# Grouping the 47th and 48th tile of nodes in a graph layer with eight experts

## What is computed

```python
hn = layernorm(x)
m = clifford_linear(hn[src] * r[edge_type]) * gate(r[edge_type]) * norm(deg_src[src], deg_dst[dst])
x = x + clifford_linear(hn + segment_sum(m, dst))
w = softmax(mean(layernorm(x)) @ Wr + br)        # the batch is one, so w is per node
y = sum over experts e of  w[e] * (relu(bn(relu(bn(layernorm(x) @ W1[e])) @ W2[e])) @ Wo[e] + bo[e])
x = x + y
```

## The kernel before

| pass | tiles | superblocks in it, at step |
|---|---|---|
| 22 | 2 | 182 to 185 at s0 to s3, 186 at s6, 187 at s9 |
| 23 | 2 | 188 at s1, 189 at s3, 190 at s6, 191 at s9 |
| 24 | 1 | 192 at s1, 193 at s3, 194 at s9 |
| 25 | 1 | 195 at s3 |
| 26 | 1 | none |

## Time and profile before

### The profile page before, as it was taken

One profiled execution on the slowest core, in us unless ns is written; L12 is line 12 of the kernel. 1 busy time (PEld: TensorE's weight loads), 2 busy tenths in 40 slices (PEclk: granted clock), 3 DMA queues, 4 the chain that ended last, 5 costly groups with the idle time before them and its releaser, 6 DMA issues.

```text
span 1869.9 us, 31246 instructions
## 1 busy us (share of the span) xinstructions
PE 1766.2 (94%) x10694; PEld 1602.7 (86%) x10694; DVE 1167.4 (62%) x2407; ACT 1310.4 (70%) x2960; POOL 1371.3 (73%) x1391
## 2 busy tenths in 40 slices
PE   5846889999999999999999999999999999999998
PEld 5835888888989989989989989998998998997888
DVE  8966566656656656656656666756665665665552
ACT  5546777768777767777768767777876776773455
POOL 5867777777777777777777777777777777777720
PEclk9977999999999999999999999999999999999999
DMA  8167344445444434434445435434444443433320
GB/s 252 52 248 229 101 135 133 109 127 136 114 117 133 127 104 131 130 105 132 126 108 135 127 107 132 129 104 129 134 115 117 133 126 105 135 109 106 105 45 6
DMA packets 93691, 231.21 MB, mean 124 GB/s; under 512 B 23338, under 2 KB 44838, under 8 KB 93595
## 3 DMA queue, kind: packets, MB, share of 16 engines
q0 software_dynamic: 60768, 168.61, 34.2%
q1 hardware_dynamic: 32012, 60.45, 10.5%
q10 hardware_dynamic: 815, 1.16, 0.2%
HBM read 216.69 MB, written 13.44 MB: 123 GB/s over the span
## 4 chain that ended last, share of the span: by engine, by line
POOL 57%; PE 19%; issue 18%; DVE 4%; DMA 2%; ACT 1%; DVEq 0%; POOLq 0%; SPq 0%
POOL H L458 36%; POOL R L458 21%; PE z L829 8%; PE y L853 4%; DVE H L1011 2%; PE pr L889 2%; PE y L740 2%; PE o L877 1%; DMA H<-h_table,src 1%; DMA h_table<-big 1%; ACT big L563 1%; PE y L805 0%; PE y L786 0%; DVE acc L1227 0%; DMA src<-in_src 0%
## 5 line engine op out<-in xcount | busy, mean ns | idle before, releaser
L458 POOL DMA_INDIRECT H<-h_table,src x784 | 817.5, 1043 | 248.3 <-issue 238.5
L458 POOL DMA_INDIRECT R<-r_table,typ x482 | 535.4, 1111 | 164.3 <-issue 163.7
L644 ACT ACTIVATE h<-z,bns 128x256 f32<-128x256 f32 (+1 forms) x864 | 418.5, 540 | 325.1 <-PE z L829 323.0
L1227 DVE SCALAR_TENSOR_TENSOR acc<-y,wg,acc 128x256 f32<-128x256 f32 x392 | 173.5, 480 | 476.3 <-PE y L853 475.1
L596 ACT ACTIVATE OH<-tb,iota_t 125x128 fp32r<-125x128 int32 x1208 | 383.7, 392 | 65.1 <-PE pr L889 49.9
L829 PE MATMUL z<-h,big 128*128 128x256 f32 (+1 forms) x1728 | 376.9, 362 | 3.2 <-ACT h L644 2.8
L829 PE MATMUL z<-hT,big 128*128 128x256 f32 (+1 forms) x1728 | 377.3, 362 | 0.7 <-ACT h L644 0.7
L853 PE MATMUL y<-big,h 128*128 128x256 f32 x1568 | 374.4, 380 | 1.7 <-DVE lg L1196 1.6
L889 PE MATMUL pr<-RH,OH 125*128 125x258 f32 x1208 | 334.8, 312 | 26.9 <-DVE H L1286 16.3
L829 PEld LDWEIGHTS z<-h,big 128*128 128x128 f32 x1728 | 306.7, 192 | 39.6 <-ACT h L644 4.4
L853 PEld LDWEIGHTS y<-big,h 128*128 128x128 f32 x1568 | 294.3, 191 | 38.8 <-issue 1.9
(11 more groups left out here) (166 smaller groups left out, 1511.9 us busy)
## 6 DMA issues: line engine op xcount, KB each, us to landing
tb<-in_typ_row SPq DMA_DIRECT2D x24, 728.0 KB
H<-h_table,src POOLq DMA_INDIRECT x784, 2.8
R<-r_table,typ POOLq DMA_INDIRECT x482, 2.8
h_table<-big SPq DMA_DIRECT2D x7, 910.0 KB, 8.6
big<-in_x SPq DMA_DIRECT2D x7, 896.0 KB, 10.9
big<-in_w SPq DMA_DIRECT2D x8, 768.0 KB, 4.8
acc<-in_x SPq DMA_DIRECT2D x22, 256.0 KB, 7.1
hxT<-in_xt SPq DMA_DIRECT2D x22, 256.0 KB
```

The source lines that it names most:

```text
L458: pool.indirect_dma_start(out=to[:, b * DX:(b + 1) * DX], out_offset=None, in_=tab, in_offset=bass.IndirectOffsetOnAxis(ap=ix[:, J * SB + ...
L644: last = s_.activation(o[:, m, 0:wide_], z_[:, m, 0:wide_], ACT.Relu, bias=bns[:, l, 1, c:c + 1], scale=bns[:, l, 0, c:c + 1])
L1227: last = v.scalar_tensor_tensor(out=acc[:, g % 3, t, :], in0=b[:, t * D:(t + 1) * D], scalar=wg[:, t, e_:e_ + 1], in1=acc[:, g % 3, t, :], ...
```

## The change

Two expressions in `sizes` change. The grouping condition `nt - t > 4` becomes `nt - t > 2`, so that tiles 46 and 47 are one group of two and only tile 48 is alone: 26 groups instead of 27. `WHOLE` becomes the end of the last group of two less one step of 8.

```diff
--- before.py
+++ after.py
@@ -32,7 +32,7 @@
     front = 2 if nt > 8 else 0
     groups, t = [], 0
     while t < nt:
-        w = 2 if t >= front and nt - t > 4 else 1
+        w = 2 if t >= front and nt - t > 2 else 1
         groups.append((t, w))
         t += w
 
@@ -56,7 +56,7 @@
         hi = max([t for t in range(nt) if edges(t, -1) < (2 * j + 2) * SE] + [lo])
         tiles.append((lo, hi))
     assert n < nt * P
-    whole = ends[twos[-1]] if twos else nsb
+    whole = max(ends[twos[-1]] - step, 0) if twos else nsb
     alike = [g for g in twos if g + 2 in twos and ends[g + 1] - ends[g] == step == ends[g + 2] - ends[g + 1]]
     loop = range(alike[0], alike[-1] + 1) if alike else range(0)
     loop = loop[:len(loop) // 2 * 2] if step % 4 == 0 else range(0)
```

## The result

The changed kernel takes **1900.77 us** (median of 4 runs, 1898.65 to 1906.57) against 1877.03 us (4 runs, 1874.71 to 1878.33): a ratio of 1.0137, 95% interval 1.0117 to 1.0157, so it is slower by 22 to 29 us. The prediction was 1904.4 us, with a range of 1897 to 1911.

What follows compares the result with a forecast made beforehand. POOL's gathers bound the tail: gate at 1794.0 + 28.3 + 46.7 + 27.8 = 1896.8 us against a span of 1869.9, +26.9; added to the median of 1877.46 this gave 1904.4 us, range 1897 to 1911.

Steps and rivals of the forecast that it cites:

- POOL is full with 73%: POOL's gathers cost 0.95 us plus an uncounted 0.30 us gap, so POOL at 73% busy practically never waits for buffers.
- The gate: Turned sums of group 24 in pass 23 wait for the gathers of superblock 195 and start at 1794.0 us.
- Rival B: POOL's slow gathers vanish where DVE is idle between landings, gate 7.0 us earlier: 1897.4 us; chance 0.12.
- the rule of shared interfaces: GpSimd and VectorE contend for SBUF; one more pair of two-input DVE operations among the gathers costs about 1 us: 1905.4 us.
- PE's idle time: In pass 23 PE waits five times for superblocks 190 to 193 and the turned sums: 29.6 us of new idle time.
- rival A: PE's clock stays at half (1.2 GHz) through the gated stretch and beyond: 1909.3 us; chance 0.16.
- Behind the gate: From the turned sums of group 24 to the next pass, now with one superblock: 28.3 us.
- the cold start: After the wait for the turned sums, 16 PE matmuls take 5.30 instead of 3.46 us, 1.84 us more.
- The pass of two and the last pass: The two-tile pass with one superblock takes 46.7 us; the last single pass and the store take 27.8 us.
- The saving of 5.0 us: Merging two one-tile passes into one of two tiles saves PE 5.0 us of its time, 53.3 less 48.3.
- Rival C: Gathers are hidden anyway and PE bounds, so only the saving of 5.0 us is left: 1872.5 us; chance 0.03.
- a slow stretch between the gates: PE's time between gates has 3 to 6 us of slack, so a stretch at slow clock there costs nothing.

Runs made afterwards that it cites:

- the kernel with the early demand alone: Kernel before, single tiles kept, but superblocks 192 and 193 demanded one group earlier, as in the changed kernel: ratio 1.0164, +30.7 us.
- the lean pair: Kernel before and changed kernel, each without the 40 relation gathers from superblock 186 on: ratios 0.9966 and 0.9959 to the kernel before.
- the run with the held product: Kernel before with DVE's product of superblock 187 and ACT's copy moved from s3 to s5 of pass 22: ratio 1.0000.

## Why the prediction was right

**The bound.** The step "POOL is full with 73%" carried everything, and the runs bear it out from both sides: 40 gathers fewer, -6.4 us; 3 more, +4.5 us (1.3 to 7.7).

**The gate.** Predicted 87.8 us behind the turned sums of group 23, measured 86.7. POOL's 64 gathers from the last one of superblock 187 to the last one of 195 took 1794.95 - 1709.56 = 85.4 us instead of 87.0:

```profile
1709.56 0.95 POOL L458 DMA_INDIRECT H<-h_table,src  x1 [0.30 <-issue]
...
1794.95 0.95 POOL L458 DMA_INDIRECT H<-h_table,src  x1 [0.30 <-issue]
```

The last landing took 4.10 us where the sum had 3.63, though the gather itself was not slow (0.95 us, where the sum had taken over 1.83): the 1.80 us from a gather's end to its landing, read from one gather, were 3.15 here. So the gate's 1.1 us are two errors of opposite sign, 1.6 us less for the gathers and 0.5 us more for the landing. Rival B (no slow gathers, 7.0 us earlier) is refuted as an extreme: 1.6 of the 7.0 us went. The 1 us that the rule of shared interfaces (the Trainium skill, GPSIMD Engine Reference, section 1, Specifications) would have added for one more product among the gathers did not appear; the total moved the other way.

**PE's idle time, a term off in kind.** Predicted: 29.6 us in five waits (11.2, 5.6, 3.2, 3.9, 5.7). Measured: 7.33, 3.49, 2.09, 3.46 and 3.28, 19.7 us, with the 1.59 before them 21.2 us. That is a third off, and by the prediction's own sign (an idle time far from 30 us) it counts against it. Of the 8.4 us missing, 1.1 are the earlier gate and the rest is slow work. The windows of PE busy, with granted clock in third place from the end:

```profile
1748.00:1803.00 55.00, 35.36 (x149) 29.57 (x148) 22.95 (x38) 14.10 (x23) 36.94 (x37) 0.84 0.40 99
1772.00:1787.00 15.00, 12.51 (x61) 10.37 (x59) 6.14 (x10) 4.03 (x7) 11.64 (x12) 1.00 0.40 110
1803.00:1830.00 27.00, 26.62 (x126) 23.09 (x125) 9.16 (x32) 11.42 (x21) 0.00 (x0) 0.94 0.00 1
```

The steps of pass 23 that I had counted as 27.1 us at full clock (from its start at 1748.47 to the gate at 1802.44, 54.0 us, less the 19.7 of waits) kept PE busy 34.3 us, 7.2 us more, at a granted clock of 0.84. Of the two levels, 1.2 and 2.4 GHz, that mean puts about a third of the stretch at the lower one. So rival A was right that bursts start at the half level. PE's timeline has the first eight matmuls of s1, s2, s3 and s4, where 1.89 us is usual:

```profile
1759.57 2.90 PE L829 MATMUL z<-hT,big 128*128 128x256 f32 x8
...
1769.39 3.11 PE L829 MATMUL z<-hT,big 128*128 128x256 f32 x8
...
1780.82 1.89 PE L829 MATMUL z<-hT,big 128*128 128x256 f32 x8
...
1791.94 3.61 PE L829 MATMUL z<-hT,big 128*128 128x256 f32 x8
```

It was wrong that the clock stays there: from 1772 to 1787, s3 included, it was full, where A had s3 at half. And it was wrong that this would reach the end: each burst still fitted into its wait, and the gate was set by the gather, as the sum had it. By the Trainium skill (TensorE: Matmul & The Clock Gate, section "HAM oscillation") the cold bursts were to be expected, and the trace agrees for four of the five: those behind 7.33, 3.49, 3.46 and 3.28 us of waiting, not the one behind 2.09. That section's example adds the penalty of every cold burst to its kernel's time; here those before the gate do not show in the time, because the wait hides them.

**Behind the gate.** 28.3 predicted, 27.7 measured, mostly because the cold start took 4.75 instead of 5.30 us. The pass of two and the last pass agree within 0.1 us.

**The saving of 5.0 us.** 4.8 us by the kernel with the early demand alone, 4.9 by the lean pair. Not all of it is PE's work, as the prediction has it: it was read from whole passes, and passes 24 and 25 of the kernel before hold 2.05 us of waits for DVE (0.93, 0.79 and 0.33) where pass 23 holds 0.72, so 1.3 of the 5.0 us are waits. What the prediction missed is that 3.5 us of it are lost again at s9 and s0 when DVE's work is placed so densely; in the changed kernel that hides behind the gathers, except for 1.59 us.

**Rival C** (gathers hidden anyway) is refuted at the place where it was to decide: DVE's idle time before the product was ended by the gathers in all five cases (31.2 us).

**The number.** 26.9 us were added to the median shown; the comparison gives 25.7 by its ratio and 23.7 by the medians. The terms that were off are small, and most have the same sign (gate -1.1, cold start behind it -0.6 us), so there is little luck in the sum. That the idle time could be a third off without harm is no luck either: the prediction says that a slow stretch between the gates costs nothing.

## What to carry to other kernels

When a group's work is merged with the next, its inputs are due one group earlier: before counting what the merged pass saves, lay the due time of each input against the time at which the queue that brings it, at its measured rate, can have it. An engine at 73% busy can be full if every instruction has a fixed gap behind it; look for idle pieces that are all equally short. And where an in-order queue prepares two steps ahead, the look-ahead itself can hold the release of work that is ready; ordering the release first brought back 14 of 26 us in the changed kernel. In the kernel before, the same idea brought nothing (ratio 1.0000), so it has to be measured each time.

## What was not expected of the hardware

Two executions drift apart in parts that are the same code: against that of the kernel before, the profiled execution of the changed kernel was 0.0 us late at the first H gather (125.92 against 125.94) and 9.6 at the last one of superblock 187 (1709.56 against 1700.01) and at the turned sums of group 23. What makes the drift was not looked into. Executions of one kernel on one chip spread by up to 12 us (1867.42 to 1879.34). The row of the first H gather in the changed kernel:

```profile
125.92 0.94 POOL L458 DMA_INDIRECT H<-h_table,src  x1 [9.68 <-DMA h_table<-big]
```

The span of one profile is then no measure of a difference under 10 us, as the run with the held product shows; stretches counted from an event that both traces share, as in the table above, are a better one.
